# Output stage of a four-layer graph network: a product of two weight matrices made on the chip, and each row tile normalised and stored on its own

## The reference

```
S = agg[:, :2*F] @ (W1_s / np.sqrt(2 * F))
V = jnp.einsum('nmi,mc->nci', agg[:, 2*F:8*F].reshape(n, 2*F, 3), W1_v) / np.sqrt(2 * F)
S = shifted_softplus(S)
S = S @ (W2_s / np.sqrt(C))
V = jnp.einsum('nci,cd->ndi', V, W2_v) / np.sqrt(C)
return jnp.concatenate([S, V.reshape(n, 3 * C)], axis=1)
...
m = jnp.mean(x, axis=axis, keepdims=True)
v = jnp.var(x, axis=axis, keepdims=True)
return (x - m) / jnp.sqrt(v + eps)
```

## Time and profile before

| | us |
|---|---|
| median of 3 runs | 2315.0 (2310.35 to 2318.41) |
| the profiled execution's own time | 2321.15 |
| its span, first to last instruction | 2319.4 |
| PE busy in the span | 2059.4 (89%) |
| DVE busy | 1605.0 (69%) |
| ACT busy | 1132.6 (49%) |
| POOL busy | 1269.8 (55%) |

### The profile page before, as it was taken

One profiled execution on the slowest core, in us unless ns is written; L12 is line 12 of the kernel. 1 busy time (PEld: TensorE's weight loads), 2 busy tenths in 40 slices (PEclk: granted clock), 3 DMA queues, 4 the chain that ended last, 5 costly groups with the idle time before them and its releaser, 6 DMA issues.

```text
span 2319.4 us, 37592 instructions
## 1 busy us (share of the span) xinstructions
PE 2059.4 (89%) x7761; PEld 1186.5 (51%) x7761; DVE 1605.0 (69%) x4532; ACT 1132.6 (49%) x3234; POOL 1269.8 (55%) x1590
## 2 busy tenths in 40 slices
PE   3788695777777999999999899999999999999986
PEld 3444342666665545455444555555555555555545
DVE  8976678888888071110313478888888888888885
ACT  0466454777774010000010267677766776776654
POOL 2577885666665656656100266666666566666530
PEclk9687797666668999999999999999999999999999
DMA  5200013111112121121000133333333333333321
GB/s 189 73 3 3 3 17 96 15 15 15 15 14 62 15 55 15 16 55 15 3 23 19 49 103 99 96 99 101 97 97 101 101 96 96 101 100 96 97 66 45
DMA packets 72178, 137.87 MB, mean 59 GB/s; under 512 B 26749, under 2 KB 37362, under 8 KB 71735
## 3 DMA queue, kind: packets, MB, share of 16 engines
q0 software_dynamic: 44704, 95.66, 17.2%
q1 hardware_dynamic: 24460, 36.11, 4.8%
q10 hardware_dynamic: 2946, 5.28, 0.6%
HBM read 114.44 MB, written 21.97 MB: 59 GB/s over the span
## 4 chain that ended last, share of the span: by engine, by line
PE 75%; DVE 16%; issue 5%; DVEq 2%; another core or an unknown queue 1%; DMA 1%; ACT 0%; POOL 0%; ACTq 0%; SPq 0%; POOLq 0%
PE ps L885 24%; PE ps L628 11%; PE ps L647 9%; PE ps L719 5%; PE ps L823 4%; PE ps L868 3%; PE ps L870 3%; PE ps L871 3%; PE ps L869 3%; DVE dense L1387 2%; DVE adj_t L1411 2%; PE ps L776 2%; DVE dense L1386 2%; DVE adj_t L1215 2%; PE ps L742 1%
## 5 line engine op out<-in xcount | busy, mean ns | idle before, releaser
L885 PE MATMUL ps<-adj_t 128*128 128x512 f32 x1288 | 615.1, 599 | 14.9 <-DVE adj_t L1622 14.9
L522 POOL DMA_INDIRECT src_table<-st_rec,st_idx x320 | 386.9, 1209 | 276.3 <-DMA st_rec<-records 184.1
L1097 ACT ACTIVATE adj_t<-adj_t 128x128 f32<-128x128 f32 x966 | 317.3, 392 | 211.2 <-DVE adj_t L1601 210.2
L569 POOL DMA_INDIRECT adj_t<-z_table,adj_t x322 | 309.9, 962 | 153.2 <-DVE adj_t L1611 67.5
L885 PEld LDWEIGHTS ps<-adj_t 128*128 128x128 f32 x1288 | 231.3, 189 | 250.5 <-issue 216.6
L510 POOL DMA_INDIRECT pair_table<-dense x192 | 234.6, 1222 | 120.7 <-issue 120.7
L776 PE MATMUL ps<-dense 128*128 128x128 f32 x832 | 236.0, 420 | 0.0
L647 PE MATMUL ps<-wring,dense 128*128 128x512 f32 (+1 forms) x480 | 209.9, 599 | 4.6 <-issue 3.2
L775 PE MATMUL ps<-dense 128*128 128x128 bf16 x416 | 116.9, 281 | 101.6 <-DVE adj_t L1411 80.1
L776 PEld LDWEIGHTS ps<-dense 128*128 128x128 f32 x832 | 195.1, 288 | 14.8
L868 PE MATMUL ps<-dense_r 128*128 128x512 f32 x322 | 200.1, 621 | 2.3 <-POOL dense_r L577 2.3
(11 more groups left out here) (276 smaller groups left out, 3659.1 us busy)
## 6 DMA issues: line engine op xcount, KB each, us to landing
src_table<-dense SPq DMA_DIRECT2D x8, 656.0 KB, 6.4
adj_t<-z_table,adj_t POOLq DMA_INDIRECT x322, 3.5
src_table<-st_rec,st_idx POOLq DMA_INDIRECT x320
records<-dense SPq DMA_DIRECT2D x1, 5000.0 KB
st_rec<-records POOLq DMA_DIRECT2D x80, 62.5 KB, 2.2
adj_t<-src_table SPq DMA_DIRECT2D x73, 64.0 KB
wring<-in_edge_attr SPq DMA_DIRECT2D x2, 1562.5 KB
wring<-in_l_w SPq DMA_DIRECT2D x3, 1024.0 KB, 6.5
```

The costliest lines, as they stand in the source:

```text
L522: g.indirect_dma_start(out=src_table, out_offset=bass.IndirectOffsetOnAxis(ap=st_idx[0:EP, k, c:c + 1].bitcast(u32), axis=0), in_=st_rec[0 ...
L569: g.indirect_dma_start(out=zg[:, s, c, :], out_offset=None, in_=z_table, in_offset=bass.IndirectOffsetOnAxis(ap=dsti[:, s, c:c + 1].bitcas ...
L885: last = mm(bank[6 + h], oh[:, c, :], msg[:, c, h * D:(h + 1) * D], start=c == c0, stop=c == c0 + count - 1)
L1097: last = A(msg[:, c, (2 + k) * P:(3 + k) * P], msg[:, c, MSG:MSG + P], ACT.Copy, scale=side[:, s, c, C_Y - ATT + k:C_Y - ATT + k + 1])
```

## The change

- At the start of L3 PE transposes W1_v (two transposes into bank 6), ACT copies them to SBUF (`w1vT`), PE multiplies them by W2_v (two products into bank 7), and ACT copies the result over `w1v`. PE's two products stand behind `filter_in(0, 1)`; ACT's first copy stands ahead of `attrs(0, 0)`, its second ahead of `hidden_hi(0, 0)`.
- In the output stage the vector half is one step: six products of 128 columns straight into `obank`, with `aT` as the stationary operand. `mixed` now signals `sv_done` after the W1_s products, then waits for `o_read` of tile t-2 and makes the six. `outputs` has one product. ACT's copy L1178 is gone.
- Each tile gets its own eps add (DVE) and its own root. For tiles 0 to 7 ACT makes exp(-0.5 ln v), two activations of 128x1, and POOL refines it by one Newton step of four small operations; for tiles 8 and 9 ACT takes Sqrt and DVE the reciprocal. DVE normalises tile t-1 behind `finish(t)`. The stores are issued by SP.

```diff
+            for t in range(NT):
+                sp_eng.wait_ge(y_ready, t + 1)
+                sp_eng.dma_start(out[t * P:t * P + rows_of(t), :], xa[0:rows_of(t), t, :]).then_inc(out_done, 16)
+            sp_eng.wait_ge(out_done, 16 * NT)
...
+            for t in range(NT - 2):
+                pool.wait_ge(guessed, t + 1)
+                r, w = rstd[:, t:t + 1], rtmp[:, t:t + 1]
+                link(g.tensor_tensor(w, r, r, ALU.mult))
+                link(g.tensor_tensor(w, w, stat[:, 1, t:t + 1], ALU.mult))
+                link(g.tensor_scalar(w, w, -0.5, 1.5, ALU.mult, ALU.add))
+                g.tensor_tensor(r, r, w, ALU.mult).then_inc(refined, 1)
...
             pe.wait_ge(l3w_ready, 2)
+            for k in range(2):
+                last = nc.tensor.transpose(bank[6][:, k * P:(k + 1) * P], w1v[:, k, :], ident[:, :])
+            last.then_inc(wT_done, 1)
             for s in range(2):
                 attrs_T(0, s)
                 filter_in(0, s)
+            pe.wait_ge(wT_copied, 1)
+            for k in range(2):
+                last = mm(bank[7][:, k * P:(k + 1) * P], w1vT[:, k, :], w2sv[:, 1, :], start=True, stop=True)
+            last.then_inc(w12_done, 1)
+            pe.wait_ge(w12_ready, 1)
             filter_out(0, 0, 0)
...
                 for k in range(2):
-                    mm(svbank[s][:, 0:P], w1s[:, k, :], aT[:, s, k, :], start=k == 0, stop=k == 1)
-                for k in range(2):
-                    last = mm(svbank[s][:, P:D], w1v[:, k, :], aT[:, s, 2 + 3 * k:5 + 3 * k, :].rearrange("p m n -> p (m n)"),
-                              start=k == 0, stop=k == 1)
+                    last = mm(svbank[s][:, 0:P], w1s[:, k, :], aT[:, s, k, :], start=k == 0, stop=k == 1)
                 last.then_inc(sv_done, 1)
+                if t >= 2:
+                    pe.wait_ge(o_read, t - 1)
+                for m in range(3):
+                    for k in range(2):
+                        last = mm(obank[s][:, (1 + m) * P:(2 + m) * P], aT[:, s, 2 + 3 * k + m, :], w1v[:, k, :], start=k == 0, stop=k == 1)
+                last.then_inc(v_done, 1)
 
             def outputs(t):
                 s = t % 2
                 pe.wait_ge(svT_ready, t + 1)
-                if t >= 2:
-                    pe.wait_ge(o_read, t - 1)
-                for m in range(KT):
-                    last = mm(obank[s][:, m * P:(m + 1) * P], svT[:, s, m * P:(m + 1) * P], w2sv[:, 0 if m == 0 else 1, :], start=True, stop=True)
-                last.then_inc(o_done, 1)
+                mm(obank[s][:, 0:P], svT[:, s, :], w2sv[:, 0, :], start=True, stop=True).then_inc(o_done, 1)
...
             nc.scalar.preload_act_table_set("natural_log_exp_and_others")
+            act.wait_ge(wT_done, 1)
+            A(w1vT, bank[6][:, 0:2 * P].rearrange("p (k n) -> p k n", k=2), ACT.Copy).then_inc(wT_copied, 1)
             attrs(0, 0)
             softplus_exp(0, 0)
             softplus_log(0, 0)
             attrs(0, 1)
+            act.wait_ge(w12_done, 1)
+            A(w1v, bank[7][:, 0:2 * P].rearrange("p (k n) -> p k n", k=2), ACT.Copy).then_inc(w12_ready, 1)
             hidden_hi(0, 0)
...
+            def root(t):
+                r = rows_of(t)
+                act.wait_ge(var_ready, 3 * NT + t + 1)
+                if t < NT - 2:
+                    link(A(rstd[0:r, t:t + 1], stat[0:r, 1, t:t + 1], ACT.Ln))
+                    A(rstd[0:r, t:t + 1], rstd[0:r, t:t + 1], ACT.Exp, scale=-0.5).then_inc(guessed, 1)
+                else:
+                    A(rstd[0:r, t:t + 1], stat[0:r, 1, t:t + 1], ACT.Sqrt).then_inc(std_ready, 1)
...
-                A(svT[:, s, P:D], sv[:, P:D], ACT.Copy).then_inc(act_sv, 1)
                 spt = sp[:, s * P:(s + 1) * P]
...
-            act.wait_ge(var_ready, 3 * NT + 1)
-            A(stat[:, 1, :], stat[:, 1, :], ACT.Sqrt).then_inc(std_ready, 1)
-            for t in range(NT):
-                act.wait_ge(y_ready, t + 1)
-                act.dma_start(out[t * P:t * P + rows_of(t), :], xa[0:rows_of(t), t, :]).then_inc(out_done, 16)
-            act.wait_ge(out_done, 16 * NT)
+                if t >= 2:
+                    root(t - 2)
+            root(NT - 2)
+            root(NT - 1)
...
-                dve.wait_ge(act_sv, 2 * t + 2)
+                dve.wait_ge(act_sv, t + 1)
+                if t >= 2:
+                    dve.wait_ge(o_done, t - 1)
...
+                v.tensor_scalar(stat[0:r, 1, t:t + 1], stat[0:r, 1, t:t + 1], EPS, None, ALU.add).then_inc(var_ready, 1)
+
+            def normalised(t):
+                r = rows_of(t)
+                y = xa[0:r, t, :]
+                if t < NT - 2:
+                    dve.wait_ge(refined, t + 1)
+                else:
+                    dve.wait_ge(std_ready, 3 * NT + t - (NT - 2) + 1)
+                    link(v.reciprocal(rstd[0:r, t:t + 1], rstd[0:r, t:t + 1]))
+                v.tensor_scalar(y, y, stat[0:r, 0, t:t + 1], rstd[0:r, t:t + 1], ALU.subtract, ALU.mult).then_inc(y_ready, 1)
 
             activated(0)
             for t in range(NT):
                 if t + 1 < NT:
                     activated(t + 1)
                 finish(t)
-            v.tensor_scalar(stat[:, 1, :], stat[:, 1, :], EPS, None, ALU.add).then_inc(var_ready, 1)
-            dve.wait_ge(std_ready, 3 * NT + 1)
-            link(v.reciprocal(stat[:, 1, :], stat[:, 1, :]))
-            for t in range(NT):
-                y = xa[0:rows_of(t), t, :]
-                r = rows_of(t)
-                v.tensor_scalar(y, y, stat[0:r, 0, t:t + 1], stat[0:r, 1, t:t + 1], ALU.subtract, ALU.mult).then_inc(y_ready, 1)
+                if t:
+                    normalised(t - 1)
+            normalised(NT - 1)
```

More of the change, by code:

```diff
@@ L246, in build @@
         bf2_r = dense_r[:, NT * D + 3 * N + P:NT * D + 3 * N + P + D]
-        svT = T1[:, 1, 0:2 * D].rearrange("p (s n) -> p s n", s=2)
+        svT = T1[:, 1, 0:2 * P].rearrange("p (s n) -> p s n", s=2)
+        w1vT = aT[:, 0, 0:2, :]
+        rstd, rtmp = [T1[:, 1, 2 * P + 16 * k:2 * P + 16 * k + NT] for k in range(2)]
         assert at[0] <= 2 * AW_COLS
@@ L343, in build @@
         t_done, aT_ready, sv_done, svT_ready, o_done, o_read = sem("t_done"), sem("aT_ready"), sem("sv_done"), sem("svT_ready"), sem("o_done"), sem("o_read")
-        act_sv = sem("act_sv")
+        act_sv, v_done, guessed, refined = sem("act_sv"), sem("v_done"), sem("guessed"), sem("refined")
+        wT_done, wT_copied, w12_done, w12_ready = sem("wT_done"), sem("wT_copied"), sem("w12_done"), sem("w12_ready")
         y_ready, out_done = sem("y_ready"), sem("out_done")
@@ L1163, in sums @@
                 if t >= 2:
-                    act.wait_ge(sv_done, t - 1)
+                    act.wait_ge(v_done, t - 1)
                 for h in range(2):
                     A(aT[:, s, 4 * h:4 * h + 4, :].rearrange("p m n -> p (m n)"), bank[4 * s + h], ACT.Copy).then_inc(aT_ready, 1)
+            def root(t):
[6 more added lines that the diff above has]
+                    A(rstd[0:r, t:t + 1], stat[0:r, 1, t:t + 1], ACT.Sqrt).then_inc(std_ready, 1)
             sums(0)
@@ L1174, in _ @@
                 if t >= 2:
-                    act.wait_ge(o_done, t - 1)
                     act.wait_ge(svT_ready, t - 1)
                 sv = bank[2 + 4 * s]
-                A(svT[:, s, P:D], sv[:, P:D], ACT.Copy).then_inc(act_sv, 1)
                 spt = sp[:, s * P:(s + 1) * P]
```

## The result

The changed kernel takes 2307.61 us (median of 8 runs, 2304.58 to 2311.62), the kernel before 2315.51 (8 runs). The ratio is 0.9969, 95% interval [0.9956, 0.9982]: 7.9 us faster, 0.31%. The forecast was 2307.1 from a gain of 7.9. The sum came out, but two of its terms were off in opposite directions, and one of them by a cause that the prediction did not know. (Each ratio is to the kernel before, with its 95% interval in brackets.)

What follows compares the result with a forecast made beforehand. PE was taken to bound the output stage at 3.50 us a tile, DVE and the stores its tail. Saving 9.5 there less 1.6 at the start of L3 takes 2315.0 to 2307.1 us, range 2304.5 to 2309.5.

Steps and rivals of the forecast that it cites:

- The start: Start of L3: the weight product and ACT's copies delay hidden_hi by 2.4 us, POOL's gathers cover 0.9; cost 1.6.
- the range given for the clock: Start of L3: the clock's rise against the first 12 filter products could move the cost by up to 0.8 either way.
- PE's sum: Output stage: PE's four groups, 0.87 + 0.45 + 1.335 + 0.22, take 2.88 us a tile, 0.62 less.
- the ring: Output stage: waits linking PE, ACT and DVE over two tiles total 6.03 us, or 3.02 a tile.
- the wait at `o_read`: Output stage: PE waits about 0.28 us in every second tile, ahead of the vector products.
- POOL's step hidden: Output stage, tiles 0 to 7: POOL's four operations take 1.6 us and are hidden by 0.3 before DVE's normalisation.
- The rival in which POOL closes the ring: Output stage: POOL's step takes 3.0 us, the stage about 3.35 a tile, total 2310.3; chance 0.15, shared with DVE.
- From first transpose to last normalisation: Output stage: summed tile by tile, the last normalisation ends at 2307.4 us, before adding the start's delay.
- The 0.4 for DVE's second wait: Output stage: 0.4 us added for the second wait ahead of `activated`, with bounds of 0 to 1.
- from the last normalisation to the end: Kernel's end: the last store and the finish take 2.5 us, bounds 2.3 to 3.2.
- a sign of being wrong: Kernel's end: more than 3.2 us from the last normalisation to the end would show the prediction wrong.
- The sum: Whole kernel: 9.5 us saved in the output stage less 1.6 lost at the start of L3, 7.9 in all.

Runs made afterwards that it cites:

- run 7: The changed kernel with ACT's output-stage order turned, activations of tile t ahead of the copies of tile t+1; output stage 40.96 us against 41.66.
- run 4: The changed kernel with POOL's Newton step made twice for tiles 0 to 7; last normalisation at 37.58 us against 37.49, output stage 42.81.
- runs 9 to 11: The changed kernel without tile 7's Newton step (output stage 40.18 us); with tile 7 by Sqrt (ratio 0.9963); that plus ACT's copies moved and output-stage order turned (0.9964).

## Why the prediction was right, step by step

- **The start.** Right in place and order: ACT's second copy ahead of `hidden_hi` put L868 off, and moving the copies takes it back. The term was 1.6 and measured 1.38 at L868: `hidden_hi` was 2.1 late, not 2.4, and POOL's gathers covered 0.7. PE's four instructions took 1.06 as forecast; it was ACT's two copies that were cheaper, 0.28 each from start to start where 0.36 was taken. Less of it reaches the output stage. Over eight profiles with the late L868 the first transpose comes at 939.6 to 940.7, mean 940.1; over six with the early one at 938.8 to 939.8, mean 939.4: 0.8. Half of the delay (1.36 on average) is gone by the end of the first scatter products, which lies 16.69 behind the last `z_table` issue on average over the late eight and 16.03 over the early six: 0.5 of it in the filter products and 0.2 at the first scatter product. The clock does not rise later when L868 is late: it does so 13.7 to 14.7 behind the issue in the late eight, 13.4 to 14.7 in the early six. So a late L868 has 8 to 10 of the first twelve filter products at 0.43 and more, from start to start, an early one 10 to 12. This was in the range given for the clock, not in the sum. With the spread within each set, 0.8 is good to a few tenths.
- **PE's sum and the ring.** 3.02 was forecast, 3.04 measured; the wait at `o_read` in every second tile is there, and run 7 removed it with the term that the ring named. The vector products take 1.34 in the first two tiles, as forecast, and 1.39 to 1.41 in the later ones that don't wait.
- **POOL's step hidden.** Right, with more room than thought: 1.02 in place of 1.6, and run 4 shows that twice the step costs 0.1. The rival in which POOL closes the ring is out.
- **From first transpose to last normalisation.** 37.8 forecast (2269.57 to 2307.4), 37.49 measured. The 0.4 for DVE's second wait was not needed: without it the forecast is 37.4.
- **The step that failed: from the last normalisation to the end.** 2.5 was taken, with bounds 2.3 to 3.2; it is 4.17, beyond the 3.2 that the prediction named as a sign of being wrong. The stores themselves keep to the forecast: SP waits 1.9, and where POOL ends early enough the whole distance is 2.7. In the changed kernel the last operation of POOL's Newton step for tile 7 starts 9.5 before the end, of which 9.08 are the rest of POOL's DRAIN, and the program can't end sooner. The prediction looked for what POOL's work costs in the ring and not for what it costs to let POOL work late.
- **The sum.** 9.5 saved in the output stage was forecast and 8.2 measured: 1.7 lost at the end, 0.3 won ahead of it; 1.6 lost at the start was forecast and 0.8 to 1.2 measured. That gives 7.0 to 7.4 by stages, and 7.9 by the medians, whose interval reaches from 4.2 to 10.2 us. That the total came within 0.5 us of the forecast is in part luck.

## What to carry to other kernels

When an edit gives a last piece of work to an engine that had long been done, ask what that engine needs to finish the program: look at the DRAIN that ends its queue, and at the distance from its last operation to the end of the span in every profile at hand; here a step of 1 us on an idle engine cost 1.5 us at the end. Where three engines are within a few per cent of each other, add up the ring of waits over the number of buffers, and not only each engine's work: it gave the pace to 1%, and the order that breaks it. Where the total's spread is larger than the effect, compare stages between events of their own. The output stage up to the last normalisation repeats to 0.1 us here (37.49 to 37.51 in the four profiles with the same output stage); the long stretch from the start of L3 to it spreads by 1.1 us over eight kernels with the same start, so there a mean of several profiles is needed.

## What the runs showed of the hardware that was not expected

- POOL's last DRAIN ends 9.08 us behind the end of POOL's last operation, in all fourteen profiles, whether that operation was one of 128x512 over 1.27 us, one of 128x1 over 0.19 or a memset of 0.10. DVE's ends 0.05 behind, PE's 0.24. The span can't end before it: from the start of POOL's last operation to the end are 9.4 to 9.5 us in the eight profiles in which nothing else was later. With POOL done in time (runs 9 to 11), the end comes 2.7 behind the last normalisation and its 196 KB store. What passes within the DRAIN no record shows, nor whether a kernel without POOL's gathers has it; both stay open.
- Linked operations of 128x1 on POOL take 0.19 us each and 0.08 to 0.09 between them, where the wider ones of the earlier trace rows had 0.18 between them.
- At the start of L3 the clock's rise to 2.4 GHz did not follow the delay of PE's filter products: 14.7 us behind the last `z_table` issue in the kernel before and in the changed one, with the first product at 8.78 and at 10.16. Of an average delay of 1.36 us some 0.5 came back in the filter products, fewer of which ran at 1.2 GHz.
